# Cross-attention with a mixture of experts: the gate logits of 29 of 32 batches formed on VectorE instead of TensorE

## The reference, cut to what matters

```
x = x + attention(layernorm(x), ctx)       # 32 batches, 112 queries x 256; ctx 375 x 192; 16 heads of 64
x = x + experts(layernorm(x))              # 8 experts, top 2

experts: router_logits = x_flat @ gate_w   # (3584 x 256) @ (256 x 8)
         router_probs  = softmax(router_logits)
         top_k_probs, top_k_idx = top_k(router_probs, 2);  shares = top_k_probs / sum(top_k_probs)
         hidden = silu(x @ gate_up_w[e][:, :512]) * (x @ gate_up_w[e][:, 512:]);  y = hidden @ down_w[e]
         output = sum over the two chosen experts of share * y
```

## Time and profile before

| | us |
|---|---|
| median of 3 runs | 1486.16 |
| lowest and highest | 1484.12, 1486.71 |
| span of the profiled execution | 1482.1 |
| PE busy | 1442.8 (97%) |
| PE loads busy | 1284.3 (87%) |
| DVE busy | 1026.8 (69%) |
| ACT busy | 811.6 (55%) |
| POOL busy | 551.1 (37%) |

### The profile page before, as it was taken

How to read it: one execution, slowest core, us unless ns; L and a number is a source line. 1 busy time by engine, 2 the same in 40 slices (tenths; PEclk the granted TensorE clock), 3 DMA queues, 4 the chain that set the end, 5 groups by cost and what they waited for, 6 DMA issues and landing times.

```text
span 1482.1 us, 38384 instructions
## 1 busy us (share of the span) xinstructions
PE 1442.8 (97%) x12134; PEld 1284.3 (87%) x12135; DVE 1026.8 (69%) x2665; ACT 811.6 (55%) x2160; POOL 551.1 (37%) x641
## 2 busy tenths in 40 slices
PE   6999999999999999999999999999998899999996
PEld 5898889898888889898988898988886788888885
DVE  5667777676777676767777776777767876666664
ACT  5555555555555555555555555555555565555553
POOL 3524344343434343434343433434326242323332
PEclk9999999999999999999999999999999999999999
DMA  9222222222222222222222222213017233333332
GB/s 272 72 67 69 74 72 74 66 76 66 73 68 77 67 77 76 91 78 78 73 66 73 68 78 66 73 41 101 27 32 283 82 64 58 51 56 51 55 55 27
DMA packets 101379, 113.82 MB, mean 77 GB/s; under 512 B 17260, under 2 KB 88156, under 8 KB 101340
## 3 DMA queue, kind: packets, MB, share of 16 engines
q1 hardware_dynamic: 88172, 94.33, 21.1%
q0 software_dynamic: 12144, 15.66, 6.1%
q10 hardware_dynamic: 1024, 3.34, 0.7%
HBM read 61.37 MB, written 51.93 MB: 76 GB/s over the span
## 4 chain that ended last, share of the span: by engine, by line
PE 92%; DVE 3%; DMA 2%; issue 1%; ACT 1%; POOL 0%; POOLq 0%; ACTq 0%; DVEq 0%
PE bank L1427 26%; PE bank L1370 21%; PE bank L1496 11%; PE bank L1472 11%; PE bank L1462 9%; PE bank L1517 6%; PE bank L1434 4%; DMA out<-y_out,dest_now 2%; PE bank L1676 1%; PE bank L1629 1%; DVE Wgu L1097 1%; PE bank L1544 1%; DVE probT L1228 1%; DMA WkU_whole<-in_L_xattn_Wkv 1%; PE bank L1534 0%
## 5 line engine op out<-in xcount | busy, mean ns | idle before, releaser
L859 ACT ACTIVATE prob<-bank,neg_max 112x375 f32<-112x375 f32 x512 | 298.7, 588 | 135.8 <-DVE neg_max L1222 135.8
L1222 DVE TENSOR_REDUCE neg_max<-bank 112x1 f32<-112x375 f32 x512 | 243.7, 538 | 15.9 <-PE bank L1462 15.7
L1472 PE MATMUL bank<-ident,prob 112*125 112x112 f32 x1536 | 214.5, 274 | 2.7 <-ACT prob L859 2.4
L1472 PEld LDWEIGHTS bank<-ident,prob 112*125 112x125 f32 x1536 | 195.9, 188 | 13.8 <-ACT prob L859 5.0
L1496 PE MATMUL bank<-probT,V 125*64 125x112 f32 x3072 | 176.3, 264 | 2.3 <-DVE probT L1228 1.5
L1496 PEld LDWEIGHTS bank<-probT,V 125*64 125x64 f32 x3072 | 148.8, 137 | 28.7 <-issue 25.5
L1005 DVE TENSOR_TENSOR K_l<-bank,K_h 128x376 fp32r<-128x376 f32 x256 | 140.2, 549 | 48.0 <-ACT K_h L815 41.6
L790 POOL DMA_INDIRECT out<-y_out,dest_now x63 | 97.8, 1552 | 200.9 <-DMA out<-y_out,dest_now 104.5
L1370 PE MATMUL bank<-Wgu,hT_h 128*128 x504 | 165.2, 409 | 2.5 <-DVE hT_l L1288 2.0
L995 DVE COPY V<-bank 125x512 f32<-125x512 f32 x96 | 66.4, 691 | 139.0 <-PE bank L1434 136.0
L813 ACT COPY V<-bank 125x512 f32<-125x512 f32 x96 | 56.3, 587 | 181.9 <-PE bank L1434 179.4
(11 more groups left out here) (209 smaller groups left out, 3867.7 us busy)
## 6 DMA issues: line engine op xcount, KB each, us to landing
bins<-pad_rows SPq DMA_DIRECT2D x29, 1032.0 KB, 5.8
inv_rows<-sums SPq DMA_DIRECT2D x126, 128.0 KB, 2.9
h_in<-bins SPq DMA_DIRECT2D x63, 129.0 KB, 2.4
Wgu<-in_L_ffn_gate_up_w SPq DMA_DIRECT2D x6, 1024.0 KB, 7.7
y_sb<-in_ctx SPq DMA_DIRECT2D x32, 187.5 KB, 2.7
y_sb<-in_ctx SPq DMA_DIRECT2D x62, 93.8 KB, 2.6
x_sb<-in_x SPq DMA_DIRECT2D x16, 224.0 KB, 2.8
x_res<-in_x SPq DMA_DIRECT2D x32, 112.0 KB, 2.4
```

Source lines behind the costliest of these rows:

```text
L859: nc.scalar.activation(prob[:, j, :], S_ps[j][0:LQ, 0:LKV], ACT.Exp, bias=neg_max[:, j:j + 1], accum_out=row_sum[:, head // HB, head % HB: ...
L1222: nc.vector.tensor_reduce(neg_max[:, j:j + 1], S_ps[j][0:LQ, 0:LKV], AX.X, ALU.max, negate=True).then_inc(max_done, 1)
L1472: last = nc.tensor.transpose(S_ps[j][0:KR, t * LQ:t * LQ + LQ], prob[:, j, t * KR:t * KR + KR], ident[0:LQ, 0:LQ])
```

## The change

For batches 0 to 28 (`by_vector(b)`) VectorE forms the logits. The gate weights are loaded broadcast to 112 partitions and brought by GpSimd into the order expert by expert (`gw_wide`). For each expert one VectorE instruction (`tensor_tensor_reduce`) multiplies `hn` with that expert's 256 weights and sums to one column of `logits`. Experts 0 to 3 are formed in step 3, ahead of VectorE's copy of V, experts 4 to 7 in the next step 0, ahead of `least`. Both `turn_hn` with `keep_hnT` and `gate_logits` are left out for these batches. ScalarE's `open_gates` moves from the end of step 0 into step 1. The new tiles lie where expert 0's weights go later, so their load waits until the gates of batch 28 are open.

```diff
+def by_vector(b):
+    return not known(b) or b < B - 3
...
+        gw_wide = nc.alloc_sbuf_tensor_at("gw_wide", [LQ, E, C], F32, offset=wgu_at)
+        gw_rows = nc.alloc_sbuf_tensor_at("gw_rows", [LQ, C, E], F32, offset=wgu_at + E * C * 4)
+        weighed = nc.alloc_sbuf_tensor_at("weighed", [LQ, 2, C], F32, offset=wgu_at + E * C * 4)
+        logits = nc.alloc_sbuf_tensor_at("logits", [LQ, E], F32, offset=wgu_at + E * C * 4 + 2 * C * 4)
...                                                                                   # SP, at the start
+            sp.dma_start(gw_rows[:].rearrange("q c e -> q (c e)"),
+                         gate_w.rearrange("(o c) e -> o (c e)", o=1).to_broadcast([LQ, C * E])).then_inc(gw_in, 16)
...                                                                                   # SP, pair(i)
                 if known(i) and i == NP - 2:
-                    load_expert(sp, 0)
...
                     if there(b, B):
                         spread_inverses(b, 0)
+                    if known(i) and i == NP - 1 and not odd:
+                        sp.wait_ge(gates_done, B - 3)
+                        load_expert(sp, 0)
...                                                                                   # GpSimd, batch 0
                         split_projection()
+                        pool.wait_ge(gw_in, 16)
+                        pool.tensor_copy(gw_wide[:], gw_rows[:].rearrange("q c e -> q e c")).then_inc(gw_ready, 1)
...                                                                                   # ScalarE, pair(i)
                         for k in made_at["mid"]:
                             evacuate(a, k)
+                        if s == 1 and there(b - 2, B):
+                            open_gates(b - 2, logits if by_vector(b - 2) else C_ps)
                         if there(b, B):
                             turned(b, s, 2)
                             turned(b, s, 3)
                         for k in made_at["late"]:
                             evacuate(a, k)
-                        if s == 0 and there(b - 2, B):
-                            open_gates(b - 2, C_ps)
...                                                                                   # VectorE
+            def weigh_experts(b, slot, first, end):
+                dve.wait_ge(hn_done, b + 1)
+                if known(b) and b == 0:
+                    dve.wait_ge(gw_ready, 1)
+                for e in range(first, end):
+                    if not known(b) or E * b + e >= 2:
+                        dve.wait_ge(parts_done, E * b + e - 1)
+                    nc.vector.tensor_tensor_reduce(out=weighed[:, e % 2, :], in0=hn[:, slot, 0, 0:C], in1=gw_wide[:, e, :],
+                                                   op0=ALU.mult, op1=ALU.add, scale=1.0, scalar=0.0,
+                                                   accum_out=logits[:, e:e + 1]).then_inc(parts_done, 1)
...
-                        if s == 3 and there(b - 1, B):
+                        if s == 3 and there(b - 1, B) and not by_vector(b - 1):
                             keep_hnT(b - 1, A_ps[1])
...
                         if s == 0 and there(b - 2, B):
-                            least(b - 2, C_ps)
+                            if by_vector(b - 2):
+                                weigh_experts(b - 2, odd, E // 2, E)
+                            least(b - 2, logits if by_vector(b - 2) else C_ps)
...
+                        if s == 3 and there(b - 1, B) and by_vector(b - 1):
+                            weigh_experts(b - 1, 1 - odd, 0, E // 2)
                         for k in made_at["V"][1:]:
                             low_part(a, k)
...                                                                                   # TensorE, pair(i)
-                            if s == 1 and there(b - 2, B):
-                                pe.wait_ge(gates_done, b - 1)
...
-                        if s == 3 and there(b - 1, B):
+                        if s == 3 and there(b - 1, B) and not by_vector(b - 1):
...
-                        if s == 0 and there(b - 2, B):
+                        if s == 0 and there(b - 2, B) and not by_vector(b - 2):
                             pe.wait_ge(lo_done, a.split(a.last_in(7, odd, 0)))
                             gate_logits(b - 2, C_ps)
...
-                            pe.wait_ge(gates_done, b - 1)
+                            if not by_vector(b - 2):
+                                pe.wait_ge(gates_done, b - 1)
                             count(b - 2)
```

More of the change, by code:

```diff
@@ L246, in attention_and_experts @@
         shared_from = place["at"]
+        gw_wide = nc.alloc_sbuf_tensor_at("gw_wide", [LQ, E, C], F32, offset=wgu_at)
+        gw_rows = nc.alloc_sbuf_tensor_at("gw_rows", [LQ, C, E], F32, offset=wgu_at + E * C * 4)
+        weighed = nc.alloc_sbuf_tensor_at("weighed", [LQ, 2, C], F32, offset=wgu_at + E * C * 4)
+        logits = nc.alloc_sbuf_tensor_at("logits", [LQ, E], F32, offset=wgu_at + E * C * 4 + 2 * C * 4)
+        assert 2 * E * C * 4 <= shared_from - wgu_at
         WqH = sb("WqH", [P, 2, HD], F32R)
@@ L370, in attention_and_experts @@
         small_in = sem("small_in")
+        gw_in, gw_ready, parts_done = sem("gw_in"), sem("gw_ready"), sem("parts_done")
         consts = sem("consts")
@@ L865, in turned, with open_gates @@
                 nc.scalar.copy(probT[:, j, :], S_ps[j][0:KR, 0:KT * LQ]).then_inc(probT_second, 1)
-            def open_gates(b, bank):
+            def open_gates(b, from_):
                 act.wait_ge(top_neg, b + 1)
-                nc.scalar.activation(gates[:], bank[0:LQ, 0:E], ACT.Exp, bias=neg_top[:, 0:1]).then_inc(gates_done, 1)
+                nc.scalar.activation(gates[:], from_[0:LQ, 0:E], ACT.Exp, bias=neg_top[:, 0:1]).then_inc(gates_done, 1)
             def copy_last_inverses():
@@ L1100, in keep_hnT, with least @@
             def keep_hnT(b, bank):
-                dve.wait_ge(hnT_made, b + 1)
+                dve.wait_ge(hnT_made, b - (B - 3) + 1)
                 nc.vector.tensor_copy(hnT[:].rearrange("p k q -> p (k q)"), bank[:, 0:2 * LQ]).then_inc(hnT_done, 1)
-            def least(b, bank):
-                dve.wait_ge(logits_made, b + 1)
-                nc.vector.tensor_reduce(neg_top[:], bank[0:LQ, 0:E], AX.X, ALU.max, negate=True).then_inc(top_neg, 1)
+            def weigh_experts(b, slot, first, end):
[8 more added lines that the diff above has]
+                                                   accum_out=logits[:, e:e + 1]).then_inc(parts_done, 1)
+            def least(b, from_):
+                if by_vector(b):
+                    dve.wait_ge(parts_done, E * b + E)
+                else:
+                    dve.wait_ge(logits_made, b - (B - 3) + 1)
+                nc.vector.tensor_reduce(neg_top[:], from_[0:LQ, 0:E], AX.X, ALU.max, negate=True).then_inc(top_neg, 1)
             def choose(b):
@@ L1538, in gate_logits @@
             def gate_logits(b, bank):
-                pe.wait_ge(hnT_done, b + 1)
-                if known(b) and b == 0:
-                    pe.wait_ge(small_in, 32)
+                pe.wait_ge(hnT_done, b - (B - 3) + 1)
                 for t in range(2):
@@ L1572, in pair @@
                         if s == 2 and there(b - 1, B):
-                            if a:
-                                how, n = a.out(a.last_in(1, odd, 1))
-                                pe.wait_ge(out_of[how], n)
-                            else:
-                                pe.wait_ge(hnT_done, b - 1)
+                            how, n = a.out(a.last_in(1, odd, 1))
+                            pe.wait_ge(out_of[how], n)
                             project(b - 1, A_ps[1])
-                        if s == 3 and there(b - 1, B):
+                        if s == 3 and there(b - 1, B) and not by_vector(b - 1):
                             for k in a.at(odd, 2, "late") if a else []:
@@ L1596, in pair @@
                             if s == 3 and there(b - 1, B):
-                                pe.wait_ge(hnT_done, b)
+                                pe.wait_ge(x2_done, b)
+                                if not by_vector(b - 1):
+                                    pe.wait_ge(hnT_done, b - (B - 3))
                             context_product(a, k, True, False)
```

## The result

The changed kernel takes 1538.31 us (median of 4 runs, 1533.08 to 1543.62), against 1486.23 for the kernel before on the same chip: a ratio of 1.036, 95% interval 1.0333 to 1.0387. It is 52 us slower, where 3 us slower was forecast and 1477 to 1504 was the range. The profiled execution has a span of 1536.4 us (before 1482.1).

What follows compares the result with a forecast made beforehand. TensorE, busy 929.44 of 930.00 us, was taken as the bound. Per batch -0.30 + 0 + 0 + 0.40 = +0.10 us, over 29 batches +2.9, giving 1489 us from 1486.2; range 1477 to 1504.

Steps and rivals of the forecast that it cites:

- Played through with a handover 0.14 before each end: Step 0: VectorE's four products alternate with GpSimd's OT_h, OT_l, x_bias; the fourth ends at 632.43, V's copy 0.45 us late.
- the prediction's own count: Step 1: TensorE loses V's copy's lateness plus its own 0.30 us lead, less a 0.35 margin.
- 29 x 0.40 = 11.6: Collision of VectorE's step 0 products with GpSimd: TensorE loses 0.40 us in step 1 of each of 29 batches.
- The gate passes: Four small passes leaving TensorE in step 0: 0.30 us gained in each batch.
- The transposes and hnT: Step 3: dropping TensorE's two transposes (bounds 0 and 0.19 us a batch) and VectorE's hnT copy brings 0.
- The multiply: VectorE's 112x256 multiply with sum from two SBUF tiles: 424 ns, estimated from the nearest fp32 rows.
- A product with its read: Multiply plus accumulator read on VectorE's queue: between 0.42 and 0.64 us a pair, taken as 0.45.
- Four products in step 3: They last 1.80 us on VectorE; V's copy comes 0.15 late, within the 0.35 margin: 0 lost.
- Rival (a): No collision between product and GpSimd in step 0; only -0.30 us a batch is left: 1477.5 us. Chance 0.25.
- (b): Rival: slow accumulator read, 0.64 us a pair, delays V's copy in steps 3 and 0: +25 us, 1511. Chance 0.12.
- (c): Rival: the product runs at half rate, 0.265 us more each; +2.0 a batch, +59 us, 1545. Chance 0.08.
- The other edits: ScalarE's gates moved to step 1, GpSimd's gate_w reordering, expert 0's delayed load: 0 each; last three batches keep TensorE's way.

Runs made afterwards that it cites:

- runs 2: Kernel before, padded with 48 semaphore increments in VectorE's loop body and the same padding ahead of the loop (295 instructions from position 197): 1486.71 us, ratio 1.0002.
- 7: Kernel before, padded so that VectorE's loop body has 295 recorded instructions from position 157, almost as in the changed kernel: 1517.31 us, ratio 1.0206.
- 3: Changed kernel, still looped, with the products of experts 4 and 5 moved ahead of the normalising of O in step 0: 1515.19 us, ratio 1.0208.
- 6: Looped changed kernel with two step 0 products ahead of the normalisation, plus 40 empty increments ahead of VectorE's loop (start 157 to 197): 1483.98 us, ratio 0.9989.
- run 5: Control: kernel before with VectorE's loop over pairs written out, nothing else changed: 1483.99 us, ratio 0.9982.
- run 8: Changed kernel, VectorE's loop written out, one of four step 0 products ahead of the normalisation, three where GpSimd works: 1475.85 us, ratio 0.9933.
- run 10: Changed kernel, VectorE's loop written out, all four products in place, GpSimd's casts held until VectorE's small maximum over the logits is done: 1479.57 us, ratio 0.9956.
- run 11: Loop-written-out version with three products where GpSimd works, plus the gate's two products kept on TensorE in step 0, unread: 1484.24 us, ratio 0.9986.
- run 12: Loop-written-out version with three products where GpSimd works, plus the two transposes kept on TensorE in step 3, unread: 1474.81 us, ratio 0.9918.
- run 1: Changed kernel with only VectorE's pair loop written out: 1506.46 us, ratio 1.0123; median 1504.9 without one slow execution.
- run 9: Changed kernel, looped, with 40 empty increments ahead of VectorE's loop (start 157 to 197): 1514.11 us, ratio 1.0162; median 1510.8 without one slow execution.

## Why the prediction was wrong

**The term that was missing.** The prediction went through what each instruction takes and waits for, and left out that VectorE's program had grown by 45 recorded instructions in the body of a loop that turns back 13 times. That is the larger half: 2.6 to 2.9 us of idle time a turn on VectorE, 13 turns, 31 us by runs 2 against 7 (1486.7 and 1517.3) and 3 against 6 (1515.2 and 1484.0), the falls of the clock behind some turns included. No step of the working had a place for it, since in the kernel before the turn costs nothing and shows in no view. What a reader could have seen is one line of the page, 18 packets in the instruction queue beside 4701 recorded VectorE instructions, which suggests that the body was not brought in again at each turn (with the loop written out, run 5, the queue moves 33); and then ask what 45 more would do. The Trainium skill, "Runtime: NRT & Kernel Launch", section "Instruction fetch mechanics", says that an engine holds two pages of 256 instructions and that a taken branch to a target outside this window waits for a fetch. The runs agree in kind: a body of 247 never waits, one of 292 to 295 waits when it starts at 157 and not at 197. That these two starts differ is what one expects when a body touches three pages or two. It is argued, not shown: which position a page begins at was not found out, since the recorded instructions are not all that the engine holds.

**The step that failed: "Played through with a handover 0.14 before each end".** The alternation is right for products 1 to 3: the two that meet GpSimd end 0.28 behind the instruction that they met (0.29 in the prediction). The fourth was put behind x_bias, ending at 632.43, as if GpSimd had nothing more: what its queue holds behind x_bias, three casts and a subtraction for a later y, was not looked at. In the kernel before they meet no product, and they start only when TensorE has made the step's V products, 0.47 us after x_bias. The prediction's own numbers take this wait away: V's copy, which waits for the same products, goes at 632.22, 0.30 earlier that is 631.92, ahead of its end of x_bias at 632.14. Now GpSimd can go from one to the next without giving way, and in 10 batches the product takes 2.27 or 3.24 us for 0.95. With V's copy 1.66 late, TensorE loses 1.66 + 0.30 - 0.35 = 1.61 in step 1 by the prediction's own count (measured 1.57), and 2.7 behind a product of 3.24 (measured 2.74). In sum 1504.9 - 1475.9 = 29 us by one product (run 8), or 25 by one wait (run 10). The forecast's 29 x 0.40 = 11.6 named the right place with two fifths of its price. For the case that it describes, run 10, it was twice too large: 29 x 0.20 = 6 by the steps, 3.7 by the times of runs 8 and 10. The fourth product ends where it was put, 3.80 us behind the start of O_now for 3.81, but V's copy begins 3.9 us behind it, not 4.05: its read and neg_top were priced too high. So the odd batches' 0.47 is a mean of short products that cost 0.25 and long ones that cost 1.57.

**What held.** The gate passes: -0.30 forecast, 8.4 us for 29 by run 11. The transposes and hnT: 0 forecast, 0 by run 12. The multiply: 424 ns forecast, 424 measured. A product with its read costs 0.35 of the queue, not 0.45, as the read lies wholly beside the next product; so rivals (b) and (c) fell: 112x256 in fp32 with an accumulator ran at the rate of the other fp32 operations from two SBUF tiles. The rule behind (c) in the Trainium skill's "Vector Engine (DVE) Microarchitecture Reference", section "Points that are easy to get wrong", is not refuted by it: it names the shape `S2S2D2_STT`, and the trace lists this product as CUSTOM_DVE_ANT_0; no run shows whether it has that shape. Four products in step 3: 0 forecast, none lost. The other edits: from the start of batch 28 to the end of the span it is 474.0 us after and 473.1 before, though this stretch holds the last turn as well, 2.1 net of the gate passes. So the delayed load and the last batches cost nothing that can be seen beside the scatter of this stretch, 471.2 to 476.6 us between the versions (they were not tried by themselves).

**The sum by the measured terms.** -8.4 for the passes, +31 for the turns, +25 to +29 for the collision: +48 to +52 from 1486.2, 1534 to 1538. Measured: 1538.3. The steps of the profiled execution say the same, summed over batches 2 to 30: -9.4 for the passes, +31.0 for the turns, +4.3 for the three falls of the clock, +26.8 in step 1, -0.7 in steps 2 and 3, together +52.0 of the 54.3 us by which the span grew. The collision's share is the softest: run 1 alone spans 1502 to 1530, and the changed kernel against run 9 leaves 27 for the turns (1538.3 and 1510.8). Rival (a), no loss by a collision, was the right number, 1477.5, for a kernel that is not this one: run 8 with 1475.9 and its control 5 with 1484.0 differ by 8.1.

**What stays open.** Where exactly the body may begin and how long it may be; why, with the casts following at once, ten batches have a long product and eleven a short one, and why all the short ones are odd; why the clock fell behind some waits of TensorE and not behind others; and whether one product ahead, looped and shifted, would reach run 8's time without writing the loop out. None was tried.

## What to carry to other kernels

Adding instructions to an engine's loop has a price that no timeline of the kernel before shows: look at the instruction queue's packets and at the idle time that "issue" ends at the loop's branch, before and after, and if they jump, shift the body by some dozens of empty instructions or write the loop out before judging the change. When an operation is put beside another engine with which it has to alternate, play through not only the instructions that the same release starts but everything that the other engine can run behind them without a wait, and ask whether such a wait will still be there once the change has made its releaser earlier. The fix may be as small as one product moved or one wait added.

## What the runs showed of the hardware

- A taken branch at the end of a body of 292 to 295 recorded instructions cost 2.3 to 2.9 us at each turn, and nothing when 40 empty ones were put ahead of it (one wait of 2.9 us came ahead of the loop instead).
- Between VectorE and GpSimd the alternation is not fair: an fp32 product from two SBUF tiles, 0.42 us by itself, was held off through x_bias and the three casts behind it (2.27 us) or these and a subtraction (3.24 us) in 10 batches, and got its turn behind x_bias at once (0.95) when the casts were held.
- VectorE's accumulator read of 82 ns lies wholly beside the next product: pairs stand 0.35 us apart.
- Behind 3 of 13 waits of TensorE at the turn the granted clock over the step was 0.86 and the step 1.4 us longer; behind the other ten it stayed at 1.00.
